# Two-layer mixed network on one core: sampling products at 64 rows in pairs, against products at 128 rows with stacked column weights

## The reference, cut to what matters

```python
ys = hh + dy + off[..., 0]
xs = ww + dx + off[..., 1]
y0, x0 = (jnp.floor(ys), jnp.floor(xs))
for oy in (0.0, 1.0):
    for ox in (0.0, 1.0):
        yy, xx = (y0 + oy, x0 + ox)
        wgt = (1.0 - jnp.abs(ys - yy)) * (1.0 - jnp.abs(xs - xx))
        valid = (yy >= 0) & (yy < H) & (xx >= 0) & (xx < W)
        g = jnp.take_along_axis(vf, idx[..., None], axis=1)
        out = out + jnp.where(valid, wgt, 0.0)[..., None] * g
return jnp.einsum('npkgc,npkg->npgc', out, mk).reshape(B, H, W, G * Cg)
```

## Time and profile before

| | us |
|---|---|
| median of three runs | 878.98 |
| lowest, highest | 876.38, 882.87 |
| the profiled execution | 881.98 |
| its span | 880.1 |
| TensorE busy | 788.3 (90%) |
| VectorE busy | 688.9 (78%) |
| GpSimd busy | 455.9 (52%) |
| ScalarE busy | 420.2 (48%) |

### The profile page before, as it was taken

The page is one execution under the profiler, slowest core; times in us unless marked ns, Lnnn a source line. Parts: engine busy times, 40 slices in busy tenths (PEclk is TensorE's granted clock), DMA queues, the critical chain, the costliest instruction groups (busy, mean ns, idle before and its releaser), DMA issues.

```text
span 880.1 us, 15474 instructions
## 1 busy us (share of the span) xinstructions
PE 788.3 (90%) x5282; PEld 572.1 (65%) x5282; DVE 688.9 (78%) x1543; ACT 420.2 (48%) x827; POOL 455.9 (52%) x421
## 2 busy tenths in 40 slices
PE   1167668999999999999999999999999999999987
PEld 0034335666777677767777777767877777777755
DVE  2477786698889887998899879988889887865454
ACT  2242233334536553647473655454745553465443
POOL 1057667565666456546755476726662855410121
PEclk9999999999999999999999999999999999999998
DMA  7333300010010000000010001000010000000000
GB/s 167 91 91 96 63 22 3 1 13 4 2 13 1 4 1 12 5 2 4 4 13 1 4 4 13 1 1 4 8 7 1 4 2 1 1 4 1 1 4 4
DMA packets 45107, 15.01 MB, mean 17 GB/s; under 512 B 40263, under 2 KB 41685, under 8 KB 45029
## 3 DMA queue, kind: packets, MB, share of 16 engines
q1 hardware_dynamic: 43869, 10.99, 6.4%
q10 hardware_dynamic: 1159, 3.04, 1.3%
HBM read 12.44 MB, written 1.57 MB: 16 GB/s over the span
## 4 chain that ended last, share of the span: by engine, by line
PE 66%; DVE 8%; issue 4%; ACT 4%; POOL 1%; DVEq 0%; ACTq 0%; POOLq 0%
PE ps_t L550 13%; PE ps_y L670 12%; PE ps_h L652 8%; PE ps_h L641 7%; PE ps_h L653 6%; PE ps_h L642 6%; PE ps_m L534 3%; DVE sb_hid L1154 2%; DVE sb_dsum L1073 2%; DVE sb_prod L1066 1%; PE ps_a L614 1%; PE ps_a L701 1%; PE ps_a L713 1%; ACT sb_hid L904 1%; ACT L904 1%
## 5 line engine op out<-in xcount | busy, mean ns | idle before, releaser
L1280 POOL TENSOR_TENSOR sb_acc<-sb_acc,sb_prod 128x512 f32<-128x512 f32 x256 | 343.2, 1360 | 178.8 <-DVE sb_prod L1066 177.9
L904 ACT ACTIVATE sb_hid<-ps_h 114x512 f32<-114x512 f32 (+1 forms) x256 | 152.7, 597 | 237.2 <-PE ps_h L642 209.7
L1154 DVE TENSOR_TENSOR sb_hid<-ps_h,sb_hid 114x512 f32<-114x512 f32 (+1 forms) x256 | 175.4, 685 | 54.0 <-PE ps_h L653 38.2
L1066 DVE TENSOR_TENSOR sb_prod<-ps_t,sb_hy 128x512 f32<-128x512 f32 x256 | 170.0, 682 | 43.2 <-PE ps_t L550 36.5
L652 PE MATMUL ps_h<-sb_xh,sb_w3s 128*114 128x256 f32 x384 | 117.7, 328 | 4.1 <-DVE sb_hid L1154 3.5
L641 PE MATMUL ps_h<-sb_xh,sb_w1s 128*114 128x256 f32 x384 | 111.7, 313 | 2.1 <-ACT sb_hid L904 2.1
L670 PE MATMUL ps_y<-sb_hid,sb_w2s 114*64 114x256 f32 x768 | 101.7, 391 | 0.6 <-DVE sb_hid L1154 0.6
L642 PE MATMUL ps_h<-sb_xl,sb_w1s 128*114 128x256 f32 x384 | 100.2, 283 | 0.0
L550 PE MATMUL ps_t<-sb_bdh,sb_hxh 64*128 64x512 f32 x288 | 80.9, 555 | 21.2 <-DVE sb_prod L1066 16.6
L653 PE MATMUL ps_h<-sb_xl,sb_w3s 128*114 128x256 f32 x384 | 99.7, 282 | 0.0
L652 PEld LDWEIGHTS ps_h<-sb_xh,sb_w3s 128*114 128x114 f32 x384 | 68.2, 178 | 37.8 <-issue 21.7
(11 more groups left out here) (197 smaller groups left out, 1473.1 us busy)
## 6 DMA issues: line engine op xcount, KB each, us to landing
sb_attn<-in_w1T SPq DMA_DIRECT2D x16, 171.0 KB, 3.0
sb_attn<-in_w3T SPq DMA_DIRECT2D x16, 171.0 KB, 3.1
sb_w2s<-in_w2T ACTq DMA_DIRECT2D x4, 342.0 KB
sb_bdh<-values SPq DMA_DIRECT2D x64, 8.0 KB, 1.8
sb_bdl<-values SPq DMA_DIRECT2D x64, 8.0 KB, 1.8
sb_attn<-in_u1T SPq DMA_DIRECT2D x4, 256.0 KB, 3.8
sb_attn<-in_u2T SPq DMA_DIRECT2D x4, 256.0 KB, 4.0
sb_xT<-in_x SPq DMA_DIRECT2D x8, 64.0 KB, 2.2
```

Source lines behind the costliest of these rows:

```text
L904: af(hid[0:ch, g % RING, :], hb[0][0:ch, :], ACT.Silu).then_inc(s_act_s, 1)
L1066: v.tensor_tensor(o.rearrange("p (g y c) -> p g y c", g=GH, y=H), tb[h][:, :].rearrange("p (g y c) -> p g y c", g=GH, y=H), w, ALU.mult).t ...
L1154: v.tensor_tensor(h, hb[1][0:ch, :], h, ALU.mult).then_inc(s_dve_hid, 1)
L1280: g.tensor_tensor(acc[n % 2][:, t, h, :], acc[n % 2][:, t, h, :], prod[:, a % PR, :], ALU.add).then_inc(s_pool_acc, 1)
```

## The change

Five things change together.

1. The high and the low part of the column weights are written to small tiles of one slot each (`hat_hi`, `hat_lo`, HR2 = 1), the high part by ScalarE instead of VectorE. Four DMAs on SP's queue per set (`stacked_weights`) then put them into `hx`: for each half h, rows 0 to 63 hold the high part of its four groups and rows 64 to 127 the low part. `hx` has two slots (HX = 2) where there were three.
2. The values are laid out for the same stacking: `bd` holds, for each part i (high or low) and half h, the block-diagonal matrix on rows 0 to 63, and one DMA (`second_rows`) copies these 64 rows to rows 64 to 127.
3. A unit of the sampling products is now one half h: two matmuls of 128 rows, stacked weights against the high and against the low values. It waits for its own bank alone. There are 576 such matmuls instead of 1152 of 64 rows.
4. `acc` has one buffer. A tap-0 product waits for the reduction of the same pixel half of the image before. `stage_hi` moves from `acc[1]` to `gb1`.
5. All five order tables are new. SP's has 124 letters, since it now has the column weights.

The order tables are left out of the diff.

```diff
-HX = 3
+HX = 2
+HR2 = 1
+SHIFT = 16 * 2 * NH
...
-    out += [("values", n), ("values_lo", n)]
+    out += [("values", n), ("values_lo", n), ("second_rows", n)]
...
-        bdh = [sb(f"bdh{i}", [P, BD], f32r) for i in range(2)]
-        bdl = [sb(f"bdl{i}", [P, BD], f32r) for i in range(2)]
+        bd = [sb(f"bd{i}", [P, 2, NH, BD], f32r) for i in range(2)]
...
-        hxh = sb("hxh", [P, HX, PIX], f32r)
-        hxl = sb("hxl", [P, HX, PIX], f32r)
+        hat_hi = sb("hat_hi", [P, HR2, PIX], f32r)
+        hat_lo = sb("hat_lo", [P, HR2, PIX], f32r)
+        hx = sb("hx", [P, HX, NH, PIX], f32r)
...
-        acc = [sb(f"acc{i}", [P, TT, NH, BD]) for i in range(2)]
+        acc = sb("acc", [P, TT, NH, BD])
...
 # SP
+            def second_rows(n):
+                sp.wait_ge(s_bd, SCATTER * (n + 1))
+                sp.dma_start(bd[n % 2][HR:P, :, :, :].bitcast(f32), bd[n % 2][0:HR, :, :, :].bitcast(f32)).then_inc(s_copy, 16)
+
+            def stacked_weights(n, k):
+                at = K * n + k
+                sp.wait_ge(s_act_hh, at + 1)
+                sp.wait_ge(s_dve_hl, at + 1)
+                if at >= HX:
+                    sp.wait_ge(s_pe_t, FIRST * (at - HX + 1))
+                for h in range(NH):
+                    for i, part in enumerate((hat_hi, hat_lo)):
+                        sp.dma_start(hx[i * HR:(i + 1) * HR, at % HX, h, :].bitcast(f32),
+                                     part[h * HR:(h + 1) * HR, at % HR2, :].bitcast(f32)).then_inc(s_hx, 16)
...
 # TensorE
             def tap(n, k, q):
                 t, h = divmod(q, NH)
-                if h:
-                    return
                 u = k * FIRST + q
-                pe.wait_ge(s_dve_hx, K * n + k + 1)
+                pe.wait_ge(s_hx, SHIFT * (K * n + k + 1))
                 if u == 0:
-                    pe.wait_ge(s_bd, SCATTER * (n + 1))
-                pe.wait_ge(s_dve_p, UNITS * n + u)
-                hi, lo = bdh[n % 2], bdl[n % 2]
-                terms = ((hxh, hi), (hxh, lo), (hxl, hi), (hxl, lo))
-                for i, (w, bd) in enumerate(terms):
-                    for g in range(NH):
-                        rows = slice(g * HR, (g + 1) * HR)
-                        last = mm(tb[g][:, :], w[rows, k % HX, t * P:(t + 1) * P], bd[rows, :], start=(i == 0), stop=(i == 3))
-                        if i == 3:
-                            last.then_inc(s_pe_t, 1)
+                    pe.wait_ge(s_copy, 16 * (n + 1))
+                if UNITS * n + u >= NH:
+                    pe.wait_ge(s_dve_p, UNITS * n + u - NH + 1)
+                w = hx[:, (K * n + k) % HX, h, t * P:(t + 1) * P]
+                mm(tb[h][:, :], w, bd[n % 2][:, 0, h, :], start=True, stop=False)
+                mm(tb[h][:, :], w, bd[n % 2][:, 1, h, :], start=False, stop=True).then_inc(s_pe_t, 1)
...
 # ScalarE
+            def weights_hi(n, k):
+                at = K * n + k
+                act.wait_ge(s_act_hat, at + 1)
+                if at >= HR2:
+                    act.wait_ge(s_hx, SHIFT * (at - HR2 + 1))
+                af(hat_hi[:, at % HR2, :], m0[:, 0:PIX], ACT.Copy).then_inc(s_act_hh, 1)
...
 # VectorE
-            def weights_hi(n, k):
-                dve.wait_ge(s_act_hat, K * n + k + 1)
-                if K * n + k >= HX:
-                    dve.wait_ge(s_pe_t, FIRST * (K * n + k - HX + 1))
-                v.tensor_copy(hxh[:, k % HX, :], m0[:, 0:PIX]).then_inc(s_dve_hh, 1)
-
             def weights_lo(n, k):
...
+                v.tensor_tensor(hat_lo[:, at % HR2, :], m0[:, 0:PIX], hat_hi[:, at % HR2, :], ALU.subtract).then_inc(s_dve_hl, 1)
...
-                if u == 0 and n >= 2:
-                    dve.wait_ge(s_dve_dr, TT * (n - 1))
-                if u == 0 and n == 1:
-                    dve.wait_ge(s_dve_w, N_PIECES)
+                if k == 0 and n >= 1:
+                    dve.wait_ge(s_dve_dr, TT * (n - 1) + t + 1)
```

More of the change, by code:

```diff
@@ L96 @@
+        xxxxxocxcc cxxxxxxxox xooo
         """,
@@ L357, in build @@
         sel32 = yg[0:CP, 0:4, :].rearrange("p a n -> p (a n)")
-        stage_hi = [acc[1][:, i, :, :].rearrange("p h n -> p (h n)").bitcast(f32r) for i in range(2)]
+        stage_hi = [gb1[:, i * EP1 // 2:(i + 1) * EP1 // 2, :].rearrange("p a n -> p (a n)").bitcast(f32r) for i in range(2)]
         hb = [ps(f"h_{i}", [P, 2 * PIX]) for i in range(2)]
@@ L457, in scatter @@
                 sp.wait_ge(s_vd, 32 * (n + 1))
-                for i, dst in enumerate((bdh, bdl)):
+                if n >= 2:
+                    sp.wait_ge(s_pe_t, UNITS * (n - 1))
+                for i in range(2):
                     for g in range(G):
-                        rows = dst[n % 2][g * W:(g + 1) * W, g % GH * H * GC:(g % GH + 1) * H * GC].bitcast(f32)
+                        h, e = divmod(g, GH)
+                        rows = bd[n % 2][e * W:(e + 1) * W, i, h, e * H * GC:(e + 1) * H * GC].bitcast(f32)
                         sp.dma_start(rows.rearrange("p (y c) -> p y c", c=GC),
                                      vd[i][:, g * GC:(g + 1) * GC].rearrange("(y x) c -> x y c", x=W)).then_inc(s_bd, 16)
+            def second_rows(n):
[11 more added lines that the diff above has]
+                                     part[h * HR:(h + 1) * HR, at % HR2, :].bitcast(f32)).then_inc(s_hx, 16)
             def next_x(n):
@@ L1250, in _ @@
             g.memset(mhalf[:, :], -0.5).then_inc(s_set, 1)
-            for tile in bdh + bdl:
-                g.memset(tile[:, :].bitcast(f32), 0.0).then_inc(s_set, 1)
+            for tile in bd:
+                for i in range(2):
+                    g.memset(tile[0:HR, i, :, :].bitcast(f32), 0.0).then_inc(s_set, 1)
             pool.wait_ge(s_set, SETS)
```

108 lines of the change are left out of this document (54 added, 54 removed).

## The result

The changed kernel takes **843.44 us** (median of 3 runs, 841.68 to 846.65) against 878.98 before: a ratio of 0.960 with an interval of 0.956 to 0.964. The forecast was 849, in a range of 829 to 887. The profiled execution of the changed kernel spans 844.7 us, that of the kernel before 880.1.

The account below looks back on a forecast made before the run. TensorE was taken to bound the long stage, chains the early one. Changes of height gave -38 us, 8 given back, the early stage 0: -30 from 882.0 makes 852, the median 3 lower, 849; range 829 to 887.

Parts of the forecast that it names:

- What bounds, and the streaming: TensorE's order sets the long stage, chains the first; a pair's matmuls stream 0.92 us before and after, gain 0.
- Wrong altogether: Sign of failure: an edge surplus that stays at one height, or streaming other than 0.23 us for two same-weight matmuls.
- Changes of height: On TensorE, 222 go, 188 of them in the stage it bounds, at 0.20 us: 38 us, 8 given back for waits.
- rival C: Freed time turns into waits for VectorE, three quarters of 38 us eaten: median 869 to 876; 0.15 for within 1%.
- The early stage: Before the first mixture, gain from banks released apart and loss from SP's order set equal: 0, ends -18 and +14.
- The sum: -38 on changes of height, 8 given back: -30 from 882.0 gives 852, median 3 lower: 849 us.
- Rival B: Early stage speeds up too: the bank-wise turn brings 2 us per set in the first image, 18 us, 831; chance 0.19.
- VectorE, -29.8 us: VectorE loses 72 copies of 0.414 us, 29.8 us, and stays 83% busy, so not the new bound by itself.
- ScalarE: ScalarE gains 72 copies of 0.37 us from PSUM, 27 us, hidden in time, each waiting for the landing before.
- The loop of one slot: High part, low part, issues and landing take 4.5 us, ceiling 9.6, covered by products at 8.5 to 10.4 per set.
- Rival D: Stacked weights arrive late in the SP-to-ScalarE loop; decides from a loop of 9 us, median 890; chance 0.22.
- Second rows: One 512 KB copy per image, 6.2 us; only the first image feels it, 1 us (0 to 14).

Follow-up runs that it names:

- e1: Kernel before with only the sampling matmuls changed: four of 128 rows per pair instead of eight of 64, old tables and waits: 844.83 us.
- e4b: Changed kernel without stacking transfers: ScalarE and VectorE write the two parts, unstacked, into three slots that TensorE reads: 836.55 us.
- e9a: Kernel before with the full-height sampling matmuls of e1 for the first image alone: 870.11 us.
- e2: e1, with a bank's unit starting when its own bank is free, for the first two images: 845.75 us.
- e3: Changed kernel with the old release in images 0 and 1: a unit of half 0 waits until both banks are empty: 863.0 us.
- e5: Changed kernel with each stacking transfer split into two of 32 rows, eight issues per set instead of four: 936.83 us.
- e13: e5 with two slots for both the high and the low part, and three product slots instead of four: 902.52 us.
- e15: Changed kernel, but ScalarE writes high parts to all 128 rows of both stacks; two low-part transfers per set, three stack slots, four product slots: 836.24 us.
- e9b: Kernel before with the full-height sampling matmuls of e1 for images 2 to 7 only: 856.57 us.
- e10b: Changed kernel with column-weight sets, from the first image's third on, going out later among the weight pieces on SP: 879.06 us.
- e6: Changed kernel with two slots for both the high and the low part, and three product slots instead of four: 852.46 us.

## Why the prediction was right, and where it was not

**What bounds, and the streaming: right.** Two full-height matmuls take the 0.23 us each that two couples' worth took. "Wrong altogether" would have been an edge that stays though all have one height. Beside the up products none did. Behind L553, the product that makes the signed distances of a set, part of it does: a group starts 0.03 us after it there and its second matmul 0.42 us later (median of 12 groups of the changed kernel between 205 and 800 us), 0.45 where streaming alone would be 0.34. Before it was 0.31 and 0.34 (behind L534, two groups), so two thirds of that edge have gone. The page "TensorEngine Tiling (Array Packing)" of the Trainium skill (Key Properties) states that changing the tiling mode drains TensorE. The trace fits it: 0.20 us per change at the 2.4 GHz level, and none once all have one height. That the time is a drain, no row shows.

**Changes of height, 188 x 0.20 = 38 us, less a fifth: the mechanism right, two terms of the sum mis-sized.** At a group the price holds. From the last up matmul before a group of four couples to the second up matmul after it, the median is 1.55 us in the kernel before (22 such groups between 205 and 800 us) and 1.16 in e1 (19 groups): 0.39 for two changes. The stage as a whole gave less. Here it is from first to last up product, before and changed:

```profile
160.57:874.01 713.44, 695.67 (x4956) 517.53 (x4956) 586.69 (x1356) 369.48 (x733) 371.04 (x348) 0.99 0.03 5
141.25:838.73 697.48, 665.93 (x4502) 517.25 (x4502) 581.53 (x1310) 386.38 (x792) 373.54 (x354) 0.99 0.15 31
```

TensorE's busy time fell by 29.7 us where I had 38, and up to 3.0 of these are the clock (17 us at the 1.2 GHz level before, 10 changed). Its idle time rose by 13.8, from 17.8 to 31.6 us, where I gave back 8. That leaves 16 of my 30. The largest wait that grew is that of L665 for VectorE, from 5.1 to 8.9 us, which is rival C's mechanism at a small size; e4b has 25.8 us idle, so the transfers and the missing slot are up to 6 of the 13.8. In e1 busy time fell by 28.5 (up to 3.3 of them the clock) and idle time rose by 4.9. That is less than 0.20 a change. Groups behind a wait or behind L553 save less than the groups between up products; what each kind adds up to over the stage isn't worked out here.

**The early stage, set to 0 with ends of -18 and +14: wrong.** It gained 19.3 us, a little beyond the end. The step that failed is the one that counted 34 changes of height there and priced none, because that stage goes by chains, and that left the clock of this stage out. A change is on the chain too where a neighbour follows at once. e9a gives 8.4 us for 24 of them, by my estimate about half edges and half clock, and e1 13.3 for all 34, with 11.7 us of TensorE's early work at the full level. e2's banks add 2.8. From e2 to e4b, which has the new tables, one accumulator, the high copy on ScalarE and three slots, it is 9.1 more, not split further; the transfers and the missing slot take 6 back.

**The sum** came near by luck in part: the two errors have opposite signs, -19 instead of 0 and -16 instead of -30, so -35 for -30. Rival B (early stage faster as well) is what happened in the early stage, with the mark at 141.25 where it said 142, but the banks, the cause that it named, bring only a part: 2.8 us in e2, 7.3 in e3.

**VectorE, -29.8 us, not the bound: right as to the bound**, 83% busy in the long stage as said. The 72 copies have gone, but its busy time fell by 9.4 us only. Other instructions of the same count take longer, the 64 of `sb_dwT` for one 40.7 us in sum instead of 35.1; why, the runs don't show. **ScalarE:** 72 copies of 381 ns, 27.4 us, priced at 27; 23 of them waited for the landing before, 28.6 us in all.

**The loop of one slot, 4.5 us: right in size (4.8), wrong in its margin.** Rival D was to decide from 9 us on. e5 shows 93 us lost at 7.2, far from all of it in the loop itself. I held the loop against the mean pace of the kernel before, 8.5 and 10.4 us. But that pace was itself set by the turn that the change opened (sets of the second image now take about 6.3 us), and a mean says nothing on sets in bursts.

The four landings of 2.0 us, issued 0.6 us apart, overlap: 4.8 us for the loop, where four in a row made 9.6. The page "DMA: Bandwidth & Descriptors" of the Trainium skill (Rules for kernel authors) says that transfers to disjoint partition halves serialize. For transfers of 64 KB issued 0.6 us apart the trace does not show it in the landing times. The advice that the page gives with it, one transfer instead of two, is borne out by e5 and e13 through the cost of the issues.

**Second rows, 6.2 us estimated:** 4.3, and TensorE waited for it once, 0.8 us in all. In e4b and e15, whose early stages are shorter, that one wait is 4.1 and 4.8 us: it is what stands next there.

## What to carry to other kernels

Where matmuls of different height alternate, count the changes, not the columns: each cost 0.2 us here at the 2.4 GHz level and 0.3 at the 1.2 one, wherever a neighbour follows at once, in a stage of chains as well as in one that TensorE fills. Hold a new loop against the smallest distance that the consumers will ask for after the change, not against the mean of before. And when a variant takes its room from another buffer, look for the wait of that buffer before judging the variant. Before dividing a gain by a count, compare TensorE's clock in both traces.

## What the runs showed of the hardware

In the changed kernel TensorE rises to 2.4 GHz earlier. From the timeline of the kernel before, neighbouring up matmuls of 256 columns, and then of the changed kernel:

```profile
151.58 0.42 PE L641 MATMUL ps_h<-sb_xh,sb_w1s 128*114 128x256 f32 x1
151.79 0.42 PE L642 MATMUL ps_h<-sb_xl,sb_w1s 128*114 128x256 f32 x1
```

```profile
135.28 0.28 PE L655 MATMUL ps_h<-sb_xl,sb_w1s 128*114 128x256 f32 x1
135.40 0.28 PE L654 MATMUL ps_h<-sb_xh,sb_w1s 128*114 128x256 f32 x1
```

0.21 us apart is the 1.2 GHz level, 0.12 the 2.4 one. The granted clock of the stretch up to 160 us reads 1.00 before and 0.80 above, the wrong way round, since the trace of the kernel before has no record of it until the first rise; the starts are the witness. The kernel before starts its full level at 167.5 us, the changed one at 133.8 (after short stretches from 51.9 us on), the same place in its program being 19 us earlier; e1 has a full stretch at 83 to 94 us, among sampling groups, before any up product.

Height alone doesn't decide it. e3 has full height everywhere and no full stretch before 142.1 us, and e9b, with the couples of the kernel before in its first two images, rises at 155.4, 12 us before that kernel. Of the 40 timed executions of the kernel before, 8 have a mean granted clock of 0.96 to 0.97 where the others have 0.99 or more, so its course differs from one execution to the next; the four fastest of all, 873.0 to 875.3 us, are among these 8. How much of a gain before the first mixture is the clock and how much the edges themselves, the runs don't separate.

The order of issue on one queue was worth as much as the whole change: 36 us for the sets' places among weight pieces (e10b). Four more issues a set of 0.6 us each cost 93 us with one slot (e5) and 50 with two (e13 against e6).
